# Two narrow attentions: scores in four 32-row tiles of TensorE, and one batch as the unit of work

## The reference, cut to what matters

```
ln_out = layernorm(hidden_states, ln1_s, ln1_b)
q, k, v = split(ln_out @ w_qkv + b_qkv)        # cross: k, v from encoder_states
scores = einsum('bhqd,bhkd->bhqk', q, k) / sqrt(16)
scores = scores * mask - 10000.0 * (1.0 - mask)
probs = softmax(scores, axis=-1)
ctx = merge_heads(einsum('bhqk,bhkd->bhqd', probs, v))
x = hidden_states + ctx @ w_ao + b_ao
```

## Time and profile before

| what | us |
|---|---|
| median of three runs | 2448.94 (2448.41 to 2450.03) |
| span of the profiled execution, first to last instruction | 2442.8 |
| what lies around the span (median less span) | 6.1 |
| PE busy | 2234.4 (91%) |
| DVE, ACT, POOL busy | 1387.9, 1014.1, 657.3 |
| self attention, first PE instruction to the last row statistics | 19.26 to 248.2 |
| cross attention, first PE instruction | 251.15 |

### The profile page before, as it was taken

How to read it: one execution, slowest core, us unless ns; L and a number is a source line. 1 busy time by engine, 2 the same in 40 slices (tenths; PEclk the granted TensorE clock), 3 DMA queues, 4 the chain that set the end, 5 groups by cost and what they waited for, 6 DMA issues and landing times. The chain is left out here.

```text
span 2442.8 us, 41130 instructions
## 1 busy us (share of the span) xinstructions
PE 2234.4 (91%) x14960; PEld 2027.3 (83%) x14960; DVE 1387.9 (57%) x2946; ACT 1014.1 (42%) x3184; POOL 657.3 (27%) x422
## 2 busy tenths in 40 slices
PE   6999899798999999999899999999798968898886
PEld 5998799797889999998789999999698846776775
DVE  5665666524545544554545554545423757888785
ACT  4777577654433333333423333333354322233332
POOL 5664766354200000000310000000053223433331
PEclk9998899899999999999999999999899967877887
DMA  4000100120000000002100000001200000000000
GB/s 148 2 0 1 44 14 14 62 78 7 5 1 4 4 4 4 4 30 78 42 5 5 4 4 4 0 4 41 62 1 9 26 5 1 5 5 5 4 5 13
DMA packets 35502, 46.28 MB, mean 19 GB/s; under 512 B 2272, under 2 KB 27456, under 8 KB 35136
## 3 DMA queue, kind: packets, MB, share of 16 engines
q1 hardware_dynamic: 35392, 44.83, 5.4%
HBM read 33.28 MB, written 2.10 MB: 14 GB/s over the span
## 5 line engine op out<-in xcount | busy, mean ns | idle before, releaser
L501 POOL TENSOR_TENSOR w_hT_lo<-arena,w_hT_hi 128x512 fp32r<-128x512 f32 x16 | 21.2, 1325 | 903.2 <-ACT w_hT_hi L661 903.2
L362 DVE TENSOR_TENSOR x_new<-x,banks 128x512 f32<-128x512 f32 x48 | 32.3, 673 | 378.0 <-PE banks L606 234.6
L693 ACT ACTIVATE arena<-banks 128x512 f32<-128x512 f32 x128 | 72.8, 595 | 416.9 <-PE banks L574 414.1
L686 ACT ACTIVATE arena<-banks,arena 128x129 f32<-128x129 f32 x512 | 180.4, 373 | 136.8 <-DVE arena L737 136.8
L606 PE MATMUL banks<-arena 128*128 128x256 f32 x1024 | 229.6, 382 | 0.0
L606 PEld LDWEIGHTS banks<-arena 128*128 128x128 f32 x1024 | 191.9, 190 | 35.4 <-issue 10.6
L756 DVE COPY arena<-banks 128x512 f32<-128x512 f32 x128 | 88.5, 692 | 210.3 <-PE banks L584 210.3
L1126 ACT ACTIVATE arena<-arena 128x128 f32<-128x128 f32 x512 | 197.8, 398 | 11.3 <-DVE arena L1176 11.3
L925 POOL TENSOR_TENSOR arena<-arena 128x512 f32<-128x512 f32 x128 | 159.9, 1272 | 109.5 <-DVE arena L1166 109.4
L116 PE MATMUL banks<-w_hT_lo,w_hi 128*128 128x256 f32 x512 | 151.8, 296 | 6.8 <-POOL w_hT_lo L501 6.8
L116 PE MATMUL banks<-w_kv_lo,w_hi 128*128 128x256 f32 x512 | 145.2, 284 | 3.8 <-DVE arena L723 3.8
(11 more groups left out here) (265 smaller groups left out, 6267.1 us busy)
## 6 DMA issues: line engine op xcount, KB each, us to landing
arena<-ctx_t SPq DMA_DIRECT2D x32, 256.0 KB, 2.5
arena<-in_L_xattn_wq SPq DMA_DIRECT2D x8, 512.0 KB, 4.3
arena<-in_L_xattn_wk SPq DMA_DIRECT2D x8, 512.0 KB, 5.2
arena<-in_L_xattn_wv SPq DMA_DIRECT2D x8, 512.0 KB, 6.2
arena<-in_L_xattn_wo SPq DMA_DIRECT2D x2, 2048.0 KB, 12.5
x<-in_x SPq DMA_DIRECT2D x4, 512.0 KB, 5.9
arena<-in_L_xattn_w SPq DMA_DIRECT2D x2, 1024.0 KB, 11.2
ctx_t<-in_ctx_t SPq DMA_DIRECT2D x1, 2048.0 KB, 12.5
```

Source lines behind the costliest of these rows:

```text
L686: done = act.activation(prob[:, b, i, :], score_tile(c, j), ACT.Exp, scale=SCALE, bias=shift[:, b, i:i + 1], accum_out=total[:, b, i:i + 1])
```

## The change

- **Scores.** q is no longer spread. `qT` and the new `kT` lie as the projections give them, eight heads on 128 partitions. The array is used as four tiles of 32 rows; each tile holds two heads. `kT` has two versions of k, one with the rows of the even heads kept and one with those of the odd heads (a column of ones and zeros, `half`), so that a product of 32 rows by 128 columns with 256 moving columns gives two heads. A batch takes eight such products: two halves `c`, and in each four tiles `r`, which write to four different banks (0 to 3). All other products still use the whole array.
- **Unit of work.** It is one batch. The scores of a batch fill four banks at once. The exponentials are still taken in groups of four heads, and their transposes go to one bank (`TR`, bank 4), which takes turns between TensorE and `copy_probs`. Banks 5 (`QV`) and 6 (`MISC`) are shared: q, v and the transposed output in one; the transposed rows, k and the output rows in the other.
- **VectorE.** The mask and the row maxima take eight heads an instruction (128x1024), the negation is part of the maximum, and the scale 0.25 has moved into q. `copy_k` is four instructions of 128x256. The bias of v is folded into a constant row, which GpSimd adds to the residual ahead of time (`add_row`); `residual` is then one addition.
- **GpSimd.** `spread_q` is gone. The masked-out term is added in pieces of 128x1024.
- **Order.** The work for the layer norm, q and k runs two pairs ahead, v one pair ahead. In the cross attention the DMA that copied a part of `less` is gone and the context is loaded two pairs ahead. `head_transpose(p - 1)` waits for `v_ok` of pair p + 1, as both use bank 5.

```diff
-        qT = sb("qT", [P, 2, H, PT])
-        kT = sb("kT", [P, 2, KC, PT])
+        qT = sb("qT", [P, 2, KC, PT])
+        kT = sb("kT", [P, 2, KC, 2, PT])
-        prob = sb("prob", [P, NHG, PAIR, HG, P])
+        prob = sb("prob", [P, 4, H, P])
...
-        CTX, OUT = bank[6], bank[7]
+        SC = core.banks[:, 0:NT, :]
+        TR, QV, MISC, CTX = bank[4], bank[5], bank[6], bank[7]
...
+            def add_row(p):
+                wait(gp, added, p)
+                gp.tensor_tensor(x_row[:, :, :], core.x[:, bass.ds(p * PAIR, PAIR), :], out_row[:, None, :].to_broadcast([P, PAIR, D]),
+                                 ALU.add).then_inc(x_row_ok, 1)
...
+                if within(p, 1):
+                    add_less(p + 1, 1 - par, 0)
+                add_row(p)
+                if within(p, 1):
+                    add_less(p + 1, 1 - par, 1)
...
+            def scores(p, par, b):
+                n = p * PAIR + b
+                wait(pe, masked, n * KC)
+                for c in range(KC):
+                    for r in range(NT):
+                        rows = slice(r * ROWS_OF, (r + 1) * ROWS_OF)
+                        mm = pe.matmul(SC[:, r, c * 2 * P:(c + 1) * 2 * P], qT[rows, par, c, b * P:(b + 1) * P],
+                                       kT[rows, par, c, :, b * P:(b + 1) * P], start=True, stop=True)
+                mm.then_inc(scored, 1)
...
+            def prob_transpose(p, par, b, g):
+                u = (p * PAIR + b) * 4 + g
+                pe.wait_ge(exp_ok, u + 1)
+                wait(pe, probT_ok, u)
+                for i in range(4):
+                    mm = pe.transpose(TR[:, i * P:(i + 1) * P], prob[:, par * 2 + b, g * 4 + i, :], core.ident[:, :])
+                mm.then_inc(trans_ok, 1)
...
+                if within(p, 3):
+                    pe.wait_ge(k_ok, p + 4)
+                else:
+                    pe.wait_ge(added, p)
...
+                    prob_transpose(p, par, b, 0)
+                    if b == 1:
+                        weigh_values(p, par, 0, 1)
+                    elif not first(p):
+                        weigh_values(p - 1, 1 - par, 1, 1)
+                    if within(p, 1):
+                        scores(p + 1, 1 - par, b)
+                    prob_transpose(p, par, b, 1)
+                    if within(p, 2):
+                        if b == 0:
+                            ln_transpose(p + 2)
+                        else:
+                            project_q(p + 2, par)
+                    weigh_values(p, par, b, 0)
+                    prob_transpose(p, par, b, 2)
+                    if b == 0 and within(p, 1):
+                        project_v(p + 1, 1 - par)
+                    if b == 1 and within(p, 2):
+                        project_k(p + 2, par)
+                    prob_transpose(p, par, b, 3)
+                    if not first(p):
+                        if b == 0:
                             head_transpose(p - 1)
-                    if g == 2 and not first:
-                        project_out(p - 1)
-                    if g == NHG - 1:
-                        if not (isinstance(p, int) and p >= NP - 2):
-                            ln_transpose(p + 2)
-                    prob_transpose(p * NHG + g, g)
+                        else:
+                            project_out(p - 1)
...
+                    exps(p, par, b, 0)
+                    if b == 1:
+                        copy_probs(p, 0, 3)
+                        if not first(p):
                             copy_head(p - 1)
-                    if g == NHG - 1 and not (isinstance(p, int) and p >= NP - 2):
-                        layer_norm(p + 2)
+                    elif not first(p):
+                        copy_probs(p - 1, 1, 3)
+                    exps(p, par, b, 1)
+                    copy_probs(p, b, 0)
+                    exps(p, par, b, 2)
+                    copy_probs(p, b, 1)
+                    if within(p, 2):
+                        if b == 0:
+                            layer_norm(p + 2, par)
+                        else:
+                            copy_q(p + 2, par)
+                    exps(p, par, b, 3)
+                    copy_probs(p, b, 2)
+                    if b == 0 and within(p, 1):
+                        copy_v(p + 1, 1 - par)
...
+            def copy_k(p, par):
+
+                dve.wait_ge(k_done, p + 1)
+                wait(dve, scored, p * PAIR - 2)
+                for t in range(KC):
+                    for e in range(2):
+                        done = dve.tensor_scalar(kT[:, par, t, e, :], MISC[:, t * PT:(t + 1) * PT], core.col(bias_k[0], bias_k[1] + t),
+                                                 half[:, e:e + 1], ALU.add, ALU.mult)
+                done.then_inc(k_ok, 1)
...
+                    if b == 0 and not (isinstance(p, int) and p < 2):
+                        residual(p - 2)
+                    if b == 0 and within(p, 2):
                         normalise(p + 2)
-                    if g == NHG - 1 and not first:
-                        new_rows(core, dve, res_ok, stat, p - 1, OUT[:, :].rearrange("p (b d) -> p b d", b=PAIR), out_ok, out_row)
+                    if b == 1:
+                        divide(p, par, 0)
+                    elif not first(p):
+                        divide(p - 1, 1 - par, 1)
+                    if within(p, 1):
+                        mask_scores(p + 1, 1 - par, b)
+                    if b == 0:
+                        row_max(p, par, 1)
+                    elif within(p, 1):
+                        row_max(p + 1, 1 - par, 0)
+                    if b == 1 and within(p, 2):
+                        copy_k(p + 2, par)
```

More of the change, by code:

```diff
@@ L928, in body @@
-            def body(p, par):
-                last = isinstance(p, int) and p == NP - 1
-                for g in range(NHG):
-                    if g < NHG - AHEAD:
-                        add_mask(p, par, g + AHEAD)
-                    elif not last:
-                        if not self_attn and g == NHG - AHEAD:
-                            gp.wait_ge(pair_ok[1 - par], (p + 1 - (1 - par)) * (DMA // 2) + DMA)
-                        add_mask(p + 1, 1 - par, g + AHEAD - NHG)
-                    if not last and g in (0, 1):
-                        spread_q(p + 1, 1 - par, g)
@@ L948, in _ @@
+            add_less(0, 0, 1)
+            gp.wait_ge(row_ok, 1)
+            for p in range(NP):
+                body(p, p % 2)
         @block.tensor
@@ L1000, in scores_ahead @@
-            def scores_ahead(p, par, g):
-                if g < NHG - AHEAD:
-                    scores(p, par, g + AHEAD)
-                elif not (isinstance(p, int) and p == NP - 1):
-                    scores(p + 1, 1 - par, g + AHEAD - NHG)
-            def prob_transpose(u, g):
-                for b in range(PAIR):
-                    pe.wait_ge(exp_ok, u * 2 + 1 + b)
-                    wait(pe, probT_ok, u * 2 - 1 + b)
-                    for i in range(HG):
-                        mm = pe.transpose(bank[4 + b][:, i * P:(i + 1) * P], prob[:, g, b, i, :], core.ident[:, :])
-                    mm.then_inc(pt_ok, 1)
@@ L1069, in _ @@
             core.wait_loaded(pe, stage, *(["w_qkv"] if self_attn else ["w_q", "w_kv"]))
             ln_transpose(0)
-            project_q(0)
-            project_v(0)
-            project_k(0)
+            project_q(0, 0)
+            project_k(0, 0)
             ln_transpose(1)
-            for g in range(AHEAD):
-                scores(0, 0, g)
-            core.wait_loaded(pe, stage, "w_out")
+            project_v(0, 0)
+            scores(0, 0, 0)
+            project_q(1, 1)
+            project_k(1, 1)
@@ L1100, in copy_v @@
             def copy_v(p, par):
-                act.wait_ge(proj_ok, p * 4 + 3)
-                act.activation(v[:, par, :, :], bank[1][:, :].rearrange("p (b d) -> p b d", b=PAIR), ACT.Copy).then_inc(v_ok, 1)
+                act.wait_ge(v_done, p + 1)
+                wait(act, pv_ok, p * 4 - 4)
+                act.activation(v[:, par, :, :], QV[:, :].rearrange("p (b d) -> p b d", b=PAIR), ACT.Copy).then_inc(v_ok, 1)
             def copy_head(p):
                 act.wait_ge(ht_ok, p + 1)
-                for k in range(KC):
-                    done = act.activation(headT[:, k, :], OUT[:, k * PT:(k + 1) * PT], ACT.Identity, bias=core.col(bias_v[0], bias_v[1] + k))
@@ L1139, in _, with exps @@
-            rstd_scalar(core, act, root)
-            layer_norm(0)
-            copy_q(0)
+                wait(act, out_ok, p)
+                act.activation(headT[:, :, :], QV[:, :].rearrange("p (k t) -> p k t", k=KC), ACT.Copy).then_inc(headT_ok, 1)
+            def exps(p, par, b, g):
+                n = p * PAIR + b
+                if g % 2 == 0:
+                    act.wait_ge(top_ok, n * KC + (g // 2 + 1))
+                for i in range(4):
+                    h = g * 4 + i
```

(17 more changed lines are left out.)

363 lines of the change are left out of this document (156 added, 207 removed).

## The result

| | before | after |
|---|---|---|
| median of four runs in one comparison, us | 2448.68 (2446.28 to 2450.03) | 2561.14 (2552.77 to 2570.22) |
| ratio to before | 1 | 1.0469 [1.0448, 1.049] |
| span of the profiled execution, us | 2442.8 | 2568.5 (its own time 2570.22) |
| six middle pairs of a stage, us (two stages) | 151.4, 151.3 | 194.8, 194.7 |
| of these at 1.2 GHz, us | 0 | 73 |

The change costs 4.7% by the ratio (112 us by the medians), where the prediction had 24 us. The profiled execution after is the longest of its four runs; its span is 125.7 us over that of before. The six middle pairs (from the first transposes of pair 0 to those of pair 6) hold 2 x 43.4 = 87 us of that, the last two pairs 31, the start of the cross attention 3, and the rest of the program, which the change doesn't touch, 5.

The account below looks back on a forecast made before the run. PE alone sets the pace. A pair goes from 25.52 to 27.0 us (20.9 work, 1.9 + 1.2 + 0.4 waits, 2.6 clock): 12 x 1.5 = +18, ends +6, so 2473 us; range 2455 to 2497, eight in ten 2428 to 2500.

Parts of the forecast that it names:

- PE's sum: PE's work in a middle pair: 25.6 - 7.15 + 2.5 = 20.9 us, without waits.
- a batch's scores: Scores of one batch in row tiles on PE: 0.86 us plus two changes of tile form at 0.2, 1.25 us.
- four tiles side by side: Scores on PE: the four row tiles run at once, each with four records of about 0.216 us.
- tiles don't overlap: Rival, chance 0.06: row tiles run one after another, scores 3.9 us a batch, 2513 us if the clock holds.
- waits absent: Rival, chance 0.10: ACT runs further ahead, PE's sum alone binds, 4.6 us a pair less, 2395 us in all.
- The pause of 1.9: PE before batch 1's first transposes waits 1.9 us for ACT's copy of v, exponentials and copy of transposes.
- The pause of 1.2 before `project_out`: In batch 1, PE waits 1.2 us for k's four copies (0.33 each) to leave the shared bank.
- Behind `ln_transpose` the products with v wait for a copy: 0.3 us: PE's only wait listed at `ln_transpose`: 0.3 us a pair, for a copy needed by the products with v.
- None of them binds by its sum: Work a pair: ACT 18.8 us, DVE about 15, POOL 11, so none of these engines sets the pace.
- a clock that holds: Rival, chance 0.18: full clock through the middle pairs, 24.4 us a pair, 2440 us in all.
- The clock: Falls to half clock in nearly every middle pair behind the 1.9 us pause, costing 2.6 us: 27.0 a pair.
- The ends of the stages: Stage starts and ends, +6 us in all; a stage's last two pairs, ACT-bound, take 2.5 us more.

Follow-up runs that it names:

- e7: The changed kernel with two `x_row` buffers, products with v widened to up to 128 columns, and v, k and output projections reordered: 2402.59 us, ratio 0.9823.
- e1: The changed kernel with `x_row` in two buffers, so `add_row` waits for the residual of one pair earlier: 2496.2 us, ratio 1.0199.
- e5: The kernel before with only its scores in 32-row tiles, two tiles at a time, old order of work kept: 2483.47 us, ratio 1.0162.
- e10: The changed kernel with only the products with v widened from 16 to up to 128 columns: 2503.49 us, ratio 1.0246.
- e2: The changed kernel with `normalise` ahead of `residual` on VectorE, GpSimd untouched: 2523.14 us, ratio 1.0309.
- e6: The changed kernel with two `x_row` buffers and products with v widened to up to 128 columns, order unchanged: 2467.96 us, ratio 1.0087.
- e8: The kernel before with scores in 32-row tiles, two at a time, and products with v widened to up to 128 columns: 2432.44 us, ratio 0.9946.

## Why the prediction was right and wrong

The direction was right, by a mechanism named for it: waits in PE's order and a clock that falls. The size was not: 2561 against 2473, beyond the range of 2455 to 2497. The largest wait was not forecast, and the falls were priced at about a third. Point by point:

- **PE's sum** (20.9 a pair), **a batch's scores** (1.25 predicted, 1.15 measured, the next group 1.07 after its start) **and four tiles side by side**: right. The rival "tiles don't overlap" is out, and "waits absent" too: that was the kernel of e7, not this one.
- **The pause of 1.9**: 0.42 + 1.39 = 1.81. The walk along the written order gave it to a tenth.
- **The pause of 1.2 before `project_out`**: 1.75. The step that I took at 0.33 a copy of k failed in size: four take 1.90, one every 0.45. It lies within the bounds given (0.25 to 0.6).
- **The step that failed**: the wait of `ln_transpose` for `normalise`, which the list of waits puts at nothing. Its only item there is "Behind `ln_transpose` the products with v wait for a copy: 0.3 us" (0.22 in e1), with GpSimd's additions priced by their sum alone ("None of them binds by its sum"). The walk priced each engine's operations alone and asked only whether the additions for batch 1 were in time; it never asked which VectorE operations run at the same time, now that `add_row` and two additions stand behind `residual`, one after the other. That made 3.7 us in each of the four pairs of a stage that have both a residual before them and rows to normalise, and by e1 it carries 65 of the 112 us, its part of the half-clock time included. Of the two pairs before the first residual, where this can't happen, the second took 25.1 at full clock, near the 24.4 that the prediction had for a clock that holds. The first took 27.5, near the 27.0 forecast, but by chance: it has no output of an earlier pair to transpose and project, and 15 us at half clock.
- **What the kernel before already showed of it**: its VectorE has one `tensor_scalar` from SBUF to SBUF in each unit (L1176), 8 elements a partition:

```profile
L1176 DVE TENSOR_SCALAR arena<-arena x64: 172/566/1289, 40.2 to 453.2; 128x8 f32<-128x8 f32 x64
...
116.61 0.70 DVE L1176 TENSOR_SCALAR arena<-arena 128x8 f32<-128x8 f32 x1
...
114.78 2.50 POOL L925 TENSOR_TENSOR arena<-arena 128x512 f32<-128x512 f32 x2 [3.94 <-DVE arena L1166]
```

  It takes 0.17 us at least and 0.57 in the median (ns in the first line), and 61 of its 64 runs end 0.03 us behind an addition of GpSimd, as this one does (117.31 and 117.28). There it cost PE nothing, but the same timing stood in the trace.
- **The clock**: falls forecast, in nearly every pair, for 3.4 to 6.8 us. They came in five of the six pairs and were two to three times as long: 10 to 17 us at half clock in each of the last four (7 us of cost in the mean), and 17.1 in the pair shown (140.52 to 147.35, and 150.76 to 161.00), which costs 8.5 where the term had 2.6. With pauses of 7.2 and PE's 20.9 that makes 36.6 of the 37.1 measured. The term took a fall to start at a pause and to end with the scores; e5 shows that with scores in row tiles there is little left in a pair that keeps the clock up, so that taking the full-array scores away is itself a cost: e5 is 1.6% slower with hardly a pause. I had the row for that (223.35 in the earlier trace rows, PE busy for 2.87 of 3.41) and used it only for a fall's place.
- **The ends of the stages**: +2.5 a stage predicted, +15.6 measured (65.1 against 49.6 and 49.3). Again mostly the clock, 43 us at half where it was 14; e10 brings it to 51.8. The cross attention's start, +2.7 predicted (2.5 in the sum), came out as +3.3.
- **The rule on pauses**: in after the clock fell behind a pause of 3.7 us and behind the pair of 0.42 and 1.39, and in e5 with no pause at all. The Trainium skill (TensorE: Matmul & The Clock Gate, "Why this matters for your kernels") warns of pauses of about 3 us and more. The fall behind 3.7 us agrees with it. By it the clock would have held in the pairs of e1 behind the first, whose longest pause is 1.75 us, and in e5, and both runs disagree.
- **Slips that change nothing**: the terms of the first pause add up to 2.83, not 2.88 (0.21 + 0.48 + 1.54 + 0.6). Six pairs before end at 194.92, not 196.66. Behind the pause at 1190 stand products of 512 columns, not 256. By its own bounds the forecast's range is about 2458 to 2503.

What in the hardware holds these operations is not shown, only the timing: L353 ends 0.02 us behind GpSimd's addition, and the first of L1184, held by the next addition, 0.15 us behind that one. The Trainium skill (SBUF — State Buffer, "Who interferes with whom") says that the two engines share a pair of SBUF ports as an exclusive lock for a whole instruction, which `tensor_scalar` from SBUF can take in its two-port modes; reductions, and operations outside those modes with at most one input from SBUF, don't need it. The trace agrees: L353 ends at 136.94, the addition at 136.92, and e2's L1203 and L1212 are not held. No run here separates the lock from another cause of the same timing.

Open: what exactly in a mix of work makes the clock hold or fall. e6, with its pauses of 0.42, 1.39 and 1.75 in a pair, falls in about one pair in three; e7, with one pause in a pair from the third on, has half clock in the first two of its middle pairs and in no later one. Open too is how much of the 112 us comes from taking the full-array scores away: no run has the new order with the old scores.

## What to carry to other kernels

When work is taken from PE, ask what the rest of it looks like to the clock: dense products that seemed pure cost may be what keeps 2.4 GHz, and where a product has few moving columns, giving it more that nobody reads may cost next to nothing (0.08 us for 16 records here) and hold the clock. When a wait is moved onto GpSimd, list the `tensor_scalar` operations of VectorE from SBUF to SBUF that its release will coincide with, since a tiny one can be held until GpSimd's addition is over (1.91 us for 0.17 here). A walk along the written order found the two pauses before batch 1 to a tenth of a microsecond and the one before `project_out` to about half of one, but not the largest, which no engine's own order contains. Find them so, then remove them by order, which here turned a change that costs 4.7% into one that saves 1.8%.

## What the runs showed of the hardware

- 16 records of 32x256 in four row tiles take 1.15 us, 1.07 to the start of the next transposes. The 16 records of 16 columns ahead of them take 1.79 to the change of tile form (132.54 to 134.33 in after), 1.70 where transposes follow (108.26 to 109.96 in the earlier trace rows).
- At full clock 16 records of 128 moving columns take 1.78 us (121.65 to 123.43 in e7), 16 of 16 columns 1.70.
- The clock fell to 1.2 GHz at the end of 3.41 us in which PE was busy throughout (e5), and held at 2.4 GHz over six pairs in which PE was idle for 4.9 of 144.5 us (e8). PE's busy share doesn't tell which.
- A `tensor_scalar` of 128x4 from SBUF to SBUF took 0.17 us alone and 1.91 beside an addition on GpSimd (L353 in e1 and after). Batch statistics (L347, L351) took the same beside it as alone, and maxima (L1212) took 1.17 each in the middle of such additions.
